# A table of both types' products ahead of the last message stage, and the last two node stages unrolled

## What is computed

```python
# L2, its node part: S, V are sums over the edges of a node; the weights of the skip depend on the node's type (0 to 3)
g_s = S @ W_dn_s * 64**-0.5;  g_v = einsum(V, W_dn_v) * 64**-0.5
sk_s = einsum(s, W_sk_s[node_species]) * 32**-0.5;  sk_v = einsum(v, W_sk_v[node_species]) * 32**-0.5
g_s = 0.5 * (g_s + sk_s);  g_v = 0.5 * (g_v + sk_v)
out = concat(silu(g_s[:, :32]), g_v * silu(g_s[:, 32:])[:, :, None])
x = layernorm(x + out)
# L3
Xs = X[src]
msg = where(edge_types == 0, Xs @ W_data.T + b_data, Xs @ W_control.T + b_control)
out = relu(segment_sum(msg, dst) + (X @ W_self.T + b_self))
x = layernorm(x + out)
```

## Time and profile before

| | |
|---|---|
| median of three runs | 19515.98 us (19462.58 to 19540.44) |
| the profiled execution's span | 19527.8 us |
| busy in it: PE, PEld | 13705.4 us (70%), 10208.8 us (52%) |
| busy in it: DVE, ACT, POOL | 11589.1 us (59%), 4277.9 us (22%), 10499.0 us (54%) |
| read from HBM, written | 933.63 MB, 367.36 MB |

### The profile page before, as it was taken

One profiled execution on the slowest core, in us unless ns is written; L12 is line 12 of the kernel. 1 busy time (PEld: TensorE's weight loads), 2 busy tenths in 40 slices (PEclk: granted clock), 3 DMA queues, 4 the chain that ended last, 5 costly groups with the idle time before them and its releaser, 6 DMA issues. The chain is left out here.

```text
span 19527.8 us, 364942 instructions
## 1 busy us (share of the span) xinstructions
PE 13705.4 (70%) x67902; PEld 10208.8 (52%) x67903; DVE 11589.1 (59%) x52990; ACT 4277.9 (22%) x11127; POOL 10499.0 (54%) x15826
## 2 busy tenths in 40 slices
PE   4467666766555557856888887689999974565555
PEld 2246666664333336745777766356666653333334
DVE  7778888885333336845665655267777754444443
ACT  7742222221111113422333332211111111000000
POOL 8878888886555553223555553045555522555560
PEclk9999999996555558978999999755555566555555
DMA  3011111111221115734555555011111110111121
GB/s 134 0 16 30 32 31 31 30 31 44 58 57 57 57 56 158 217 102 114 155 154 153 155 152 123 10 35 39 39 39 39 39 25 24 40 41 41 41 41 18
DMA packets 1925133, 1295.55 MB, mean 66 GB/s; under 512 B 1295114, under 2 KB 1679741, under 8 KB 1925096
## 3 DMA queue, kind: packets, MB, share of 16 engines
q1 hardware_dynamic: 1600808, 593.17, 13.5%
q0 software_dynamic: 324288, 701.98, 13.2%
HBM read 933.63 MB, written 367.36 MB: 67 GB/s over the span
## 5 line engine op out<-in xcount | busy, mean ns | idle before, releaser
L977 DVE TENSOR_TENSOR agg<-agg,edge_psA 128x256 f32 x4992 | 2078.2, 416 | 2042.1 <-issue 1567.3
L951 POOL DMA_INDIRECT edge_sv<-tab,edge_ix x1664 | 1569.1, 943 | 2169.6 <-DVE edge_ix L1332 1735.8
L951 POOL DMA_INDIRECT edge_xs<-tab,edge_ix x1664 | 1589.5, 955 | 1615.0 <-DVE edge_ix L1592 1141.0
L951 POOL DMA_INDIRECT edge_fs<-tab_a,edge_ix x1664 | 1573.0, 945 | 1634.7 <-DVE edge_ix L1044 1187.0
L1611 PE MATMUL edge_psA<-edge_oh,edge_xs 128*128 128x256 f32 x3328 | 1580.5, 626 | 1146.1 <-DVE agg L977 877.6
L610 POOL DMA_INDIRECT by_src<-send_row,send_pl x1664 | 1615.3, 971 | 1257.4 <-issue 1097.3
L662 PE MATMUL send_psX<-x_res,send_ohT 128*128 x3328 | 1315.5, 499 | 1188.2 <-ACT send_ohT L643 1078.8
L460 POOL DMA_INDIRECT records<-place_pl,place_place x1568 | 1614.4, 1030 | 550.9 <-issue 515.4
L1611 PEld LDWEIGHTS edge_psA<-edge_oh,edge_xs 128*128 128x128 f32 x3328 | 922.3, 306 | 1803.8 <-issue 935.1
L662 PEld LDWEIGHTS send_psX<-x_res,send_ohT 128*128 128x128 f32 x3328 | 833.9, 311 | 1758.4 <-issue 1758.4
L1398 PE MATMUL edge_psA<-edge_oh,edge_m 128*128 128x128 f32 x6656 | 1593.2, 421 | 0.7 <-DVE edge_m L1367 0.7
(11 more groups left out here) (310 smaller groups left out, 31165.4 us busy)
## 6 DMA issues: line engine op xcount, KB each, us to landing
edge_fd<-tab_b SPq DMA_DIRECT2D x1664, 128.0 KB
max_row<-by_src SPq DMA_DIRECT2D x392, 258.0 KB
running<-max_back POOLq DMA_DIRECT2D x392, 256.0 KB
records<-count_tmpl SPq DMA_DIRECT2D x64, 858.0 KB
send_pl<-records SPq DMA_DIRECT2D x832, 66.0 KB
edge_pl<-records SPq DMA_DIRECT2D x832, 50.0 KB
place_pl<-in_edge_attr SPq DMA_DIRECT2D x781, 50.0 KB
by_src<-send_row,send_pl POOLq DMA_INDIRECT x1664
```

Source lines behind the costliest of these rows:

```text
L951: pool.indirect_dma_start(rows[b % len(rows)][:, k, :], None, table[:], bass.IndirectOffsetOnAxis(ap=ix[b][:, k:k + 1], axis=0)).then_inc( ...
L977: v.tensor_tensor(block, block, psA[b % 2][:, k * 2 * D:(k + 1) * 2 * D], ALU.add).then_inc((s_half if k == 0 else s_acc)[b], 1)
```

## The change

`tab_3` becomes twice as wide: after the norm of layer 2, node2 multiplies each node's rows by both types' weights of layer 3, adds their biases and stores 256 columns. Seen as 25088 rows of 128, row 2n + t is the message of node n for type t. edge3 computes 2 n + t once for all edges and gathers that row, one indirect DMA a column as before, so that a column needs one one-hot and one add of 128 columns. Groups have four columns (`G` = 4), of which `DEEP` = 8 are in flight; ScalarE copies `ix` and the one-hot keys; four block numbers are loaded at once; TensorE takes the one-hot as weights. `agg` starts from `b_self`. Ahead of edge3 the order of VectorE's queue is: keys, row numbers, then the fill of `agg`.

node2 and node3 have no loop: 25 units (`NU`) of up to four blocks are written out as a pipeline. In node2 three of the unit's masked transposes come ahead of the gathered products; `mask` and the copy of the rows are merged (one multiply makes 4 x 32 columns, a type each); the statistics of the norm come from `bn_stats` and the square roots from batches of five units; scale and offset are applied by ScalarE; rows and table of a unit follow six steps later (`LAG`). node3 keeps only the product of the own rows.

```diff
+UN = 4
+UNITS = [(4 * u, min(4, NBLK - 4 * u)) for u in range(-(-NBLK // UN))]
+def pair_stats(v, st, y, b0, n):
+
+    for p in range(n // 2):
+        last = v.bn_stats(st[:, b0 // 2 + p, :], y[:, 2 * p:2 * p + 2, :].rearrange("p k d -> p d k"))
+    return last
...
 def node2_phase(nc, S, a, agg):
     with Phase(nc, "node2") as ph:
-        M, Z = 32, 160
-        NS = 4
...
+        LAG, BATCH, NT3, NXT = 6, 5, 3, 5
...
+        xm = ph.sbs("xm", NS, [P, UN, P])
+        xT = ph.sbs("xT", NXT, [P, UN, P])
+        psT = [ph.bank(f"psT{k}") for k in range(3)]
+        psZ = [ph.bank(f"psZ{k}") for k in range(2)]
+        psY = [ph.bank(f"psY{k}") for k in range(3)]
...
+            for j, (b0, n) in enumerate(UNITS):
+                sp.wait_ge(s_t3, sum(k // 2 for _, k in UNITS[:j + 1]))
+                sp.dma_start(tab[:, b0:b0 + n, :], agg[:, b0:b0 + n, :]).then_inc(s_out, 16)
+            sp.wait_ge(s_out, 16 * NU)
...
+            def gathered(u):
+                b0, n = UNITS[u]
+                wait(pe, s_zc, u)
+                for k in range(n):
+                    ps, o = z_of(k)
+                    pe.matmul(ps[:, o:o + 3 * M], agg[:, b0 + k, 0:D], wd0[:], start=(k % 2 == 0), stop=False,
+                              skip_group_check=True)
...
+            pe.wait_ge(s_wc, 1)
+            for s in range(NU + LAG):
+                if s < NU:
+                    for c in range(3):
+                        masked(s, c)
+                    gathered(s)
+                    skip(s, 0)
+                    masked(s, 3)
+                    skip(s, 1)
+                if s >= LAG:
+                    rows(s - LAG)
+                if s < NU:
+                    skip(s, 2)
+                    skip(s, 3)
+                if s >= LAG:
+                    table(s - LAG)
...
+            def skips(u):
+                b0, n = UNITS[u]
+                act.wait_ge(s_use, NS * u + NS)
+                for h in range(n // 2):
+                    z = psZ[h][:, 0:2 * Z].rearrange("p (k c) -> p k c", k=2)
+                    o = agg[:, b0 + 2 * h:b0 + 2 * h + 2, 0:Z]
+                    act.activation(o[:, :, 0:2 * M], z[:, :, 0:2 * M], ACT.Silu)
+                    last = act.activation(o[:, :, 2 * M:], z[:, :, 2 * M:], ACT.Copy)
+                last.then_inc(s_zc, 1)
...
+            act.wait_ge(s_zero, 4)
+            for s in range(NU + LAG):
+                if s >= LAG:
+                    norm(s - LAG)
+                if s < NU:
+                    for c in range(NS):
+                        evict(s, c)
+                if s >= LAG:
+                    evict(s - LAG, "x")
+                if s < NU:
+                    skips(s)
+                for r in range(-(-NU // BATCH)):
+                    if s == batch(r)[1] + 1:
+                        roots(r)
...
+            def masked(u, c):
+                b0, n = UNITS[u]
+                if u > 0:
+                    v.wait_ge(s_T, turn[u - 1, c] + 1)
+                rows = S.x[:, b0:b0 + n, 0:M] if c == 0 else S.x[:, b0:b0 + n, M + c - 1:M + c + 3 * M - 3:3]
+                v.tensor_tensor(xm[c][:, 0:n, :].rearrange("p k (t m) -> p k t m", t=NS),
+                                rows.rearrange("p k (a m) -> p k a m", a=1).to_broadcast([P, n, NS, M]),
+                                mask[:, b0:b0 + n, :].rearrange("p k (t a) -> p k t a", a=1).to_broadcast([P, n, NS, M]),
+                                ALU.mult).then_inc(s_xm, 1)
...
+            for c in range(NS):
+                masked(0, c)
+            for s in range(NU + LAG):
+                if s < NU:
+                    gated(s)
+                if s + 1 < NU:
+                    masked(s + 1, 0)
+                    masked(s + 1, 1)
+                if s < NU:
+                    stats(s)
+                if s + 1 < NU:
+                    masked(s + 1, 2)
+                    masked(s + 1, 3)
+                for r in range(-(-NU // BATCH)):
+                    if s == batch(r)[1] + 1:
+                        scales(r)
+                if s >= LAG:
+                    table(s - LAG)
 
 
...
 def edge3_phase(nc, S, a, agg):
     with Phase(nc, "edge3") as ph:
-        DEEP = 8
-        ix = ph.sbs("ix", DEEP, [P, G2], I32)
-        xs = ph.sbs("xs", DEEP, [P, G2, D])
-        oh = ph.sbs("oh", 2, [P, G2, 2, P])
-        psA = [ph.bank(f"psA{k}") for k in range(2)]
-        s_turn, s_zero = (ph.sem(n) for n in ("s_turn", "s_zero"))
-        s_half, s_acc = ph.sems("s_half", DEEP), ph.sems("s_acc", DEEP)
+        DEEP, G, NPS, NOH = 8, 4, 4, 4
+        GT = NT // G
+        b_self = ph.sb("b_self", [P, D])
+        ix = ph.sbs("ix", DEEP, [P, G], I32)
+        dl = ph.sbs("dl", DEEP, [P, G])
+        ys = ph.sbs("ys", DEEP, [P, G, D])
+        oh = ph.sbs("oh", NOH, [P, G, P])
+        psA = [ph.bank(f"psA{k}") for k in range(NPS)]
+        s_turn, s_b, s_row, s_add = (ph.sem(n) for n in ("s_turn", "s_b", "s_row", "s_add"))
         s_ix, s_got, s_oh, s_C = (ph.sems(n, DEEP) for n in ("s_ix", "s_got", "s_oh", "s_C"))
         block = ph.block()
-        GT = NT // G2
+        table = S.tab_3.rearrange("n (t d) -> (n t) d", t=2)
+
+        @block.sync
+        def _(sp):
+            sp.dma_start(b_self[:], a.L3_gnn_b_self.rearrange("(a d) -> a d", a=1).to_broadcast([P, D])).then_inc(s_b, 16)
+
+        @block.scalar
+        def _(act):
+            act.wait_ge(s_row, 2)
+
+            def step(s, g, b, r):
+                wait(act, s_C[b], r)
+                act.activation(ix[b][:], S.e_src[:, bass.ds(g * G, G)], ACT.Copy)
+                act.activation(dl[b][:], S.e_dl[:, bass.ds(g * G, G)], ACT.Copy).then_inc(s_ix[b], 1)
+            runs(GT, [0], DEEP, act, step)
 
         @block.gpsimd
         def _(pool):
-            runs(GT, [0], DEEP, pool,
-                 lambda s, g, b, r: gather_on(pool, b, ix, xs, S.tab_3, s_ix, s_got, s_turn, r))
+            def step(s, g, b, r):
+                pool.wait_ge(s_ix[b], r + 1)
+                pool.sem_inc(s_turn, 1)
+                for k in range(G):
+                    pool.indirect_dma_start(ys[b][:, k, :], None, table,
+                                            bass.IndirectOffsetOnAxis(ap=ix[b][:, k:k + 1], axis=0)).then_inc(s_got[b], 16)
+            runs(GT, [0], DEEP, pool, step)
 
         @block.vector
         def _(v):
-            v.memset(agg[:], 0.0).then_inc(s_zero, 1)
-
-            v.scalar_tensor_tensor(S.e_dl[:], S.e_dl[:], -1.0, S.e_dl0[:], ALU.add, ALU.subtract).then_inc(s_zero, 1)
-            v.wait_ge(s_zero, 2)
+            v.tensor_tensor(S.e_dl0[:], S.e_dl[:], S.e_dl0[:], ALU.not_equal).then_inc(s_row, 1)
+            v.wait_ge(s_row, 1)
+            v.scalar_tensor_tensor(S.e_src[:], S.e_src[:], 2.0, S.e_dl0[:], ALU.mult, ALU.add).then_inc(s_row, 1)
+            v.wait_ge(s_b, 16)
+            v.tensor_scalar(agg[:, :, 0:D], b_self[:].rearrange("p (a d) -> p a d", a=1).to_broadcast([P, NBLK, D]), 1.0,
+                            None, ALU.mult).then_inc(s_add, 1)
             at = []
 
             def step(s, g, b, r):
-                o, n = two_before(b, r, DEEP)
+                k = s // 2
                 if s == 0:
-                    wait(v, s_got[b], r * 16 * G2)
-                    wait(v, s_C[b], r)
-                    v.tensor_scalar(ix[b][:], S.e_src[:, bass.ds(g * G2, G2)], 1.0, None, ALU.mult).then_inc(s_ix[b], 1)
-                elif s == 1:
-                    at[:] = load_blocks(v, S, g)
-                elif s == 3:
-                    wait(v, s_C[o], n)
-                    one_hot(v, oh[b % 2][:, :, 0, :], S, S.e_dl0, g)
-                    one_hot(v, oh[b % 2][:, :, 1, :], S, S.e_dl, g).then_inc(s_oh[b], 1)
+                    at[:] = nc.values_load_multi_w_load_instructions(
+                        S.blk[0:1, bass.ds(g * G, G)], engines=[mybir.EngineType.DVE], min_val=0, max_val=NBLK - 1)[1]
+                elif s % 2 == 1:
+                    if k == 0:
+                        v.wait_ge(s_ix[b], r + 1)
+                        o, n = before(b, r, NOH, DEEP)
+                        wait(v, s_C[o], n)
+                    hot = v.tensor_scalar(oh[b % NOH][:, k, :], S.iota[:], dl[b][:, k:k + 1], None, ALU.is_equal)
+                    if k == G - 1:
+                        hot.then_inc(s_oh[b], 1)
                 else:
-                    add_to_block(v, agg, at, psA, b, r, s // 4, s_C, s_half, s_acc, DEEP)
-            runs(GT, [0, 6, 6, 4, 6], DEEP, v, step)
+                    k -= 1
+                    rows = agg[:, bass.ds(at[k], 1), 0:D].rearrange("p a c -> p (a c)")
+                    if k == 0:
+                        v.wait_ge(s_C[b], r + 1)
+                    v.wait_ge(s_add, g * G + k + 1)
+                    v.tensor_tensor(rows, rows, psA[b % NPS][:, k * D:(k + 1) * D], ALU.add).then_inc(s_add, 1)
+            runs(GT, [2, 0, 2, 0, 2, 0, 2, 0, 2], DEEP, v, step)
 
         @block.tensor
         def _(pe):
```

(42 more changed lines are left out.)

427 lines of the change are left out of this document (231 added, 196 removed).

## The result

The changed kernel takes **18850.4 us** in the median of four runs (18839.6 to 18882.2), the kernel before, measured beside it, 19510.8 us (median of four, 19462.6 to 19540.4): a ratio of 0.968, 95% interval 0.966 to 0.970. The direction was right, the size was not: 660 us are saved and not 1100, and 18850 lies above the range's top of 18700.

A forecast was written before the change was run, and what follows sets the result against it. VectorE, handing GpSimd its indices late, was taken to bound edge3; node2 and node3 were chains. Savings of 578 + 176 + 347 = 1101 us from 19527.8 give 18427, or 18415 from the median run; range 18310 to 18700.

The forecast's parts named there:

- The gather's 1.25 us: In edge3, GpSimd left alone issues one gather every 1.25 us, so 1664 of them take 2080 us.
- the start beside the first gathers: In edge3, `agg` is filled beside the first gathers, so 4.3 us instead of 23.7 us stand ahead of them.
- the VectorE turn: In edge3, VectorE needs 3.3 to 5.0 us for four columns, 3.7 taken, against GpSimd's 5.0 us.
- (e): In edge3, TensorE's four matmuls of 128 columns take 2.5 us at most at half clock and stay hidden.
- 34 us for collisions: In edge3, 34 us added to 2096 us for collisions on the way, with gathers stretched by 20 ns, giving 2130 us.
- the prediction's own sign: In edge3's profile after the change, a gather spacing above 1.35 us makes the prediction fall.
- VectorE stays the bound: Rival in edge3: slow queue stretches make VectorE's turn 5.3 us, 6.6 at worst; whole 18540 or 19080 us; chance 0.16.
- the 578 us: Time edge3 was to save, from 2708.0 to 2130 us, by GpSimd no longer waiting for a late VectorE.
- the forecast's 11 and 15: In node2, one pipeline step takes 11 us near the full clock, 15 us at the half clock.
- Gathers stretched or delayed by one-hots: Rival in edge3: one-hots hold up GpSimd, 0.1 or 0.28 us a gather; whole 18580 or 18880 us; chance 0.09.
- Nodes as weak as chains: Rival in node2 and node3: pipelines no better than half-clock chains, 440 and 150 us; whole 18590 us; chance 0.07.
- Starved unrolled stages: Rival in the unrolled stages: feeding TensorE new instructions at 0.7 us each makes the whole 20765 us; chance 0.02.

## Why the prediction was right and wrong

**Edge3, bounds and mechanism: right.** The gather's 1.25 us, the start beside the first gathers, the VectorE turn (3.7 us forecast, 3.24 measured without hindrance), no stretched gathers from scalar one-hots (945 to 950 ns against 955 before): on a chip without stretches the stage takes 2124 us.

**Edge3, the step that failed** is the one behind (e): eight groups of buffers "in which a late VectorE is made up for", and its price, 34 us for collisions; on the first chip the stage ended 446 us above the 2130. By the prediction's own sign it falls, too: gathers came every 1.55 us in the mean (2576.5/1664), above its limit of 1.35. A cover helps against a delay that ends and leaves room behind it. At 3.24 us a turn against 5.0 VectorE wins back 1.76 us a turn, and the stretches take 6.19 - 3.24 = 2.95 us a turn in the mean. By this sum no depth makes that up (it was not tried with more). The prediction had the number for it: 0.82 us for two columns of old work. It put this into a rival as 1.64 for four and gave it 0.16; 5.3 us a turn was too low for the first chip, where it was 6.19, and the rival's worst, 6.6, a little too high. So the rival "VectorE stays the bound" is what came, at 18850 between its two prices of 18540 and 19080, though what holds VectorE is not its own work. One argument against that rival was weaker than it looked: the row read as edge2's covers 3620 us, and edge2 takes 3123 of them, the rest is mostly node1.

**What the 578 us were.** The prediction read the earlier trace rows as a fault of the kernel: VectorE late with `ix`. The runs show 2708 us on one chip and 2142 on another for the same code. Of the 628 us between the gathers' 2080 and 2708, 566 are gone on a chip without stretches (2708 - 2142), and on the first chip the changed kernel still pays 452 (2576 - 2124). The 578 us forecast could be won only in part: without stretches there were 18. The trace had a warning that the prediction wrote down and left ("What causes them the trace does not say"): a load that takes 699 ns instead of 302 was a cost of unknown cause, and the sum let it go with the work beside it.

**node2: the chain was right, the clock was not.** The gated part starts once a step:

```profile
15948.24 0.67 DVE L1672 TENSOR_TENSOR agg<-agg 128x384 f32<-128x384 f32 x1 [12.20 <-ACT agg L1615]
15965.26 0.68 DVE L1672 TENSOR_TENSOR agg<-agg 128x384 f32<-128x384 f32 x1 [12.19 <-ACT agg L1615]
...
16006.67 0.70 DVE L1672 TENSOR_TENSOR agg<-agg 128x384 f32<-128x384 f32 x1 [5.79 <-ACT agg L1615]
16018.49 0.69 DVE L1672 TENSOR_TENSOR agg<-agg 128x384 f32<-128x384 f32 x1 [5.76 <-ACT agg L1615]
```

```profile
15880.14:15965.26 85.12, 69.55 (x320) 66.68 (x320) 24.16 (x45) 16.42 (x41) 0.00 (x0) 0.50 0.00 0
...
15983.03:16030.31 47.28, 41.05 (x308) 36.98 (x307) 24.19 (x45) 21.43 (x53) 0.00 (x0) 0.97 0.13 45
16030.31:16048.09 17.78, 15.80 (x75) 14.70 (x75) 6.39 (x14) 8.08 (x17) 0.00 (x0) 0.61 0.08 30
```

17.02 us a step at a granted clock of 0.50 (half speed, 1.2 GHz), 11.82 at 0.97 (near the full 2.4): the forecast's 11 and 15 were short by 0.8 and 2. (Its own terms give 15.7 at the half clock: 5.9 us of TensorE doubled and 3.9 of the rest.) The first six of 24 intervals run at the half clock, in the first five with TensorE busy for 69.55 of 85.12 us, and three later ones take 17.6 to 17.8 us again, one of them shown at a mean of 0.61. The 24 take 331.8 us instead of 264: 20 by the base, 32 by the first six, 16 by the later ones, among them two of 13.1 us, in which a change of ScalarE's function table (1.28 us), forecast as hidden, is on the path. The split by cause is an estimate from these lengths. Start (30 us to the first gated part) and tail (25) were as forecast or less.

**node3: better than forecast** (67 against 89), with TensorE near its full clock:

```profile
18820.00:18872.00 52.00, 37.59 (x274) 32.18 (x272) 51.47 (x142) 48.14 (x132) 0.00 (x0) 0.95 0.33 102
```

VectorE is busy for 99% of this window; a unit takes 2.11 us (adds at 18821.68 and 18823.79), the sum of its operations, and TensorE at 0.95 is never late. The forecast had 2.8 us by taking TensorE's half clock of the stage before the change.

**The other rivals.** Gathers stretched or delayed by one-hots: not with the scalar form. Nodes as weak as chains: no, though node2, at 387 between 334 and 440, went half of that way. Starved unrolled stages: no; the records of instruction fetches go from 12 packets on their queue to 29 and node2's steps are accounted for without them.

```profile
q8 instruction: 29, 0.48, 0.0%
```

## What to carry to other kernels

An engine that idles at "issue" while its own queue instructions take several times their usual length may be held by something the kernel does not own: run the unchanged kernel on another chip before pricing an edit that is to win that time back, and see whether the trace has all the signals that the program raises. Buffers cover a late engine only up to its spare rate (here 1.76 us a turn), not a mean loss above it. And an experiment that confirms every theory has tested none: look first at a stage that no edit touched (edge1 here).
